# Bulk loads and stores of x issued by ScalarE, and the row of the maxima sent before the reciprocals are spread

## What is computed

```python
x = x + _layernorm(_L0_attn_ref(_layernorm(x), W_qkv, b_qkv, W_out, b_out))
x = x + _layernorm(_L0_ffn_ref(_layernorm(x), weight, alpha, bias))
# attention: softmax(causal(q k^T / sqrt(8))) v, then W_out
# ffn: einsum('bsd,od->bso', input, ternary(weight) * alpha) + bias
```

## Time and profile before

| | |
|---|---|
| median of 3 runs | 443.43 us |
| the profiled execution | 442.58 us |
| its span | 440.8 us |
| busy: PE, DVE, ACT, POOL | 375.1, 357.8, 329.5, 301.7 us |
| DMA queue of SP: packets, MB | 70880, 37.70 |
| DMA queue of ACT: packets, MB | 1336, 0.66 |
| mean granted clock of TensorE | 0.96 |

### The profile page before, as it was taken

How to read it: one execution, slowest core, us unless ns; L and a number is a source line. 1 busy time by engine, 2 the same in 40 slices (tenths; PEclk the granted TensorE clock), 3 DMA queues, 4 the chain that set the end, 5 groups by cost and what they waited for, 6 DMA issues and landing times.

```text
span 440.8 us, 19219 instructions
## 1 busy us (share of the span) xinstructions
PE 375.1 (85%) x7430; PEld 279.4 (63%) x7430; DVE 357.8 (81%) x1148; ACT 329.5 (75%) x609; POOL 301.7 (68%) x584
## 2 busy tenths in 40 slices
PE   0635898899999989998999999999989999998541
PEld 0323666567777767776777777777767777665230
DVE  5845775799999897998999998989989988985542
ACT  0412675788899887998989998898889889778521
POOL 2633332576888876888888887878887777656855
PEclk9998898999999998999999999999999999999955
DMA  7298545533344433333344334353345334511161
GB/s 192 42 122 96 91 104 116 123 82 84 80 85 85 83 76 74 83 82 76 75 87 85 83 85 86 80 123 84 85 84 126 83 82 85 113 45 33 56 188 48
DMA packets 72306, 39.58 MB, mean 90 GB/s; under 512 B 13048, under 2 KB 68056, under 8 KB 72216
## 3 DMA queue, kind: packets, MB, share of 16 engines
q1 hardware_dynamic: 70880, 37.70, 40.9%
q10 hardware_dynamic: 1336, 0.66, 0.6%
HBM read 13.67 MB, written 4.72 MB: 42 GB/s over the span
## 4 chain that ended last, share of the span: by engine, by line
PE 32%; DMA 25%; SPq 13%; issue 9%; DVE 8%; ACT 8%; POOL 5%; POOLq 0%; ACTq 0%; DVEq 0%
DMA QS<-MpT 9%; PE ps_st L795 7%; PE ps_mx L846 7%; DMA den<-Y 7%; PE ps_y L819 7%; SPq L260 6%; DMA rec_dram<-rec 4%; DMA QS<-part 4%; SPq L270 3%; ACT PT L427 3%; PE ps_w L875 3%; DVE M L627 3%; PE ps_w L916 3%; PE ps_w L905 2%; POOL rstd L358 2%
## 5 line engine op out<-in xcount | busy, mean ns | idle before, releaser
L627 DVE TENSOR_REDUCE M<-ps_mx 128x2 f32<-128x512 f32 (+3 forms) x352 | 211.9, 633 | 32.2 <-PE ps_mx L846 31.6
L427 ACT ACTIVATE PT<-ps_st 128x1024 f32<-128x1024 f32 (+1 forms) x192 | 162.6, 883 | 21.9 <-PE ps_st L795 15.8
L846 PE MATMUL ps_mx<-KS,QS 112*64 112x128 bf16 (+2 forms) x2560 | 136.9, 226 | 13.2 <-DMA QS<-part 10.3
L846 PEld LDWEIGHTS ps_mx<-KS,QS 112*64 112x64 bf16 x2560 | 94.1, 112 | 47.2 <-DVE M L627 13.1
L795 PE MATMUL ps_st<-QS,KS 114*64 114x256 bf16 (+1 forms) x1024 | 103.6, 304 | 13.6 <-DMA QS<-MpT 12.7
L358 POOL TENSOR_TENSOR rstd<-vareps,mhalf 128x2 f32<-128x2 f32 x128 | 91.7, 717 | 10.0
L819 PE MATMUL ps_y<-PT,VB 128*32 128x256 f32 (+3 forms) x2048 | 90.4, 303 | 0.4 <-ACT PT L427 0.3
L795 PEld LDWEIGHTS ps_st<-QS,KS 114*64 114x64 bf16 x1024 | 48.5, 111 | 20.5 <-DMA QS<-MpT 17.9
L819 PEld LDWEIGHTS ps_y<-PT,VB 128*32 128x32 f32 x2048 | 49.6, 109 | 12.9 <-issue 5.7
L400 POOL TENSOR_TENSOR rest<-QK,part 128x512 f32<-128x512 f32 x32 | 38.8, 1214 | 24.4 <-ACT part L456 24.4
L386 POOL TENSOR_TENSOR yn<-Y,rden 128x512 f32<-128x512 f32 x32 | 40.7, 1272 | 16.6 <-DMA rden<-rec_dram 16.6
(11 more groups left out here) (63 smaller groups left out, 492.2 us busy)
## 6 DMA issues: line engine op xcount, KB each, us to landing
QS<-part SPq DMA_DIRECT2D x192, 64.0 KB
rden<-rec_dram SPq DMA_DIRECT2D x32, 256.0 KB
X<-in_x SPq DMA_DIRECT2D x7, 512.0 KB, 5.4
out<-X SPq DMA_DIRECT2D x7, 512.0 KB, 4.4
KS<-part SPq DMA_DIRECT2D x32, 96.0 KB
KS<-part SPq DMA_DIRECT2D x32, 64.0 KB
KS<-part SPq DMA_DIRECT2D x32, 32.0 KB
QS<-MpT SPq DMA_DIRECT2D x32, 16.0 KB
```

The lines of the kernel that those rows point to most:

```text
L427: nc.scalar.activation(PT[(b * CHUNKS + n) % TILES][:, 0:512 * banks], ps_st[n % 2][:, 0:banks, :].rearrange("p a c -> p (a c)"), ACT.Exp, ...
L627: nc.vector.tensor_reduce(M[b % 2][:].rearrange("p k g i -> p (k g) i")[:, 2 * kv:2 * kv + pairs, i], ps_mx[(b * BANKS + n) % 2][:, 0:pair ...
L846: last = pe.matmul(ps_mx[(b * BANKS + n) % 2][64 * one:64 * one + 64, at:at + w], q[:, h, BL * i:BL * i + BL], k[:, kv, blocks, :], start= ...
```

## The change

Two things are done. First, `load_x` and `store_x` go from SP to ACT, with their DMAs on ACT's queue. On ACT the load stands first in a step; the store stands behind `take_xn1(t)` and takes batch t-10 in the place of t-21. ACT's loop gets two steps more and a last wait for all stores; SP's loop ends at t = 36. Second, SP's step sends the row of the maxima before it spreads the reciprocals.

```diff
         @block.sync
-            def load(g):
-                sp.dma_start(rows(g), xv[bass.ds(g, 1)].rearrange("n p r d -> (n p) r d")).then_inc(s_x, 16)
...
             def step(t):
-                load_x(t)
+                send_max(t - 3)
                 spread_rec(t - 5)
-                send_max(t - 3)
                 q_rows(t - 1, 1, 1)
                 q_rows(t - 1, 1, 5)
                 k_rows(t - 1, 2)
                 q_rows(t - 1, 2, 0)
-                store_x(t - 21)
                 send_den(t - 4)
...
-            for t in range(B + 21):
+            for t in range(B + 5):
                 step(t)
-
-            sp.wait_ge(s_store, 16 * (B // GRP - 1 + GRP))
...
         @block.scalar
+            def load_x(t):
+                g = t + 1
+                if g < B // GRP:
+
+                    act.wait_ge(s_x, g * 16)
+                    act.dma_start(rows(g), xv[g]).then_inc(s_x, 16)
+
+            def store_x(b):
+                if on(b) and (b % GRP == GRP - 1 or b >= B - GRP):
+
+                    act.wait_ge(s_fin, b + 1)
+                    if b < B - GRP:
+                        g = b // GRP
+                        act.dma_start(ov[g], rows(g)).then_inc(s_store, 16)
+                    else:
+                        at = (b - (B - GRP)) * TT
+                        act.dma_start(ov[B // GRP - 1, :, at:at + TT, :], X[:, TT * b:TT * b + TT, :]).then_inc(s_store, 16)
...
             def step(t):
+                load_x(t)
                 take_xn1(t)
+                store_x(t - 10)
                 exp(t - 4, 5)
...
-            for t in range(B + 8):
+            for t in range(B + 10):
                 step(t)
+
+            act.wait_ge(s_store, 16 * (B // GRP - 1 + GRP))
```

More of the change, by code:

```diff
@@ L224, in _ @@
             xv = x.rearrange("(n b) (j p) d -> n p (b j) d", b=GRP, p=128)
-            ov = out.rearrange("(n b) (j p) d -> n p (b j) d", b=GRP, p=128)
-            def rows(g):
-                return X[:, bass.ds(g * (GRP * TT), GRP * TT), :]
-            def load(g):
-                sp.dma_start(rows(g), xv[bass.ds(g, 1)].rearrange("n p r d -> (n p) r d")).then_inc(s_x, 16)
             sp.dma_start(X[:, 0:TT, :], xv[0, :, 0:TT, :]).then_inc(s_x0, 16)
@@ L239, in _ @@
                 sp.dma_start(dst[:], src).then_inc(s_late, 16)
[L241 to L246, removed]
             def rows_free(b):
@@ L418, in _, with rows @@
         def _(act):
+            xv = x.rearrange("(n b) (j p) d -> n p (b j) d", b=GRP, p=128)
+            ov = out.rearrange("(n b) (j p) d -> n p (b j) d", b=GRP, p=128)
+            def rows(g):
+                return X[:, bass.ds(g * (GRP * TT), GRP * TT), :]
             def exp(b, n):
```

## The result

The changed kernel takes 473.36 us in the median of 4 runs (469.52 to 476.2), against 442.77 us for the kernel before in its 4 runs: a ratio of 1.071, interval 1.064 to 1.078. It is 30.6 us slower. The forecast was 437.0 us, with a range to 448.

The account below looks back on a forecast made before the run. PE was taken to set the pace, with DVE close behind. Terms -9.5 - 1.7 + 4.2 - 2.4 + 3.3 + 0.5 = -5.6 us against 442.58 gave 437.0 us, range 428 to 448.

Parts of the forecast that it names:

- What is queued behind the row pays: On SP's queue, rden, part sends and den go out later behind the row: 0.2 us a step, +4.2 us, bounds 0 and +23.
- The 2.9 us of the earlier trace: Issue-to-use time of one den transfer of 16 KB without the spreading before it, compared with the row's 4.17 us.
- the 0.8 us for each store: Three group stores on SP directly ahead of a den each delay it by 0.8 us; moving them saves 2.4 us.
- the 1.0 us a step that was taken: DVE's distance behind PE in a steady step: a step takes 11.50 us, of which DVE needs 10.5.
- slower: Rival at send_max: SP stands at the row while rden and den wait; 0.85 us a step, 450.7 us, chance 0.15.
- The row goes first: Row sent before the spreading, 1.3 to 1.9 us earlier: PE's waits for it give -9.5 us, the slow clock stretch -1.7.
- Stores and loads on ACT: Stores meeting the spreading +3.3 us, stores no longer ahead of den on SP -2.4, ACT's issues of loads and stores +0.5.
- the cover named for its issues: ACT's waits for QK, 23.5 us together, hide its load and store issues; without that cover they would cost 9.2 us.
- the signs listed for "wrong": Most steps: yn waits for rden or reciprocal over 0.8 us for den; ACT's QK wait gone; or MpT waits that stay.

Follow-up runs that it names:

- e3_small: Changed kernel with the spreading of the reciprocals cut from 256 KB to 16 KB, most of the division left out: 448.99 us, ratio 1.014.
- e7_issue: Kernel before with one more DMA of 16 bytes on SP behind the row in each of 32 steps: 454.69 us, ratio 1.021.
- e2_move: Changed kernel with the two sends back in their old order, so only loads and stores move to ACT's queue: 451.37 us, ratio 1.008.
- e5_row_act: Kernel before with the row of the maxima sent by ACT on its own queue, behind the layer norm: 466.61 us, ratio 1.033.
- e6_row_act_move: Changed kernel with the row of the maxima sent by ACT on its queue, behind the layer norm: 460.20 us, ratio 1.031.
- e9_row_act_first: Kernel before with the row sent by ACT directly behind the copy of MpT, ahead of the layer norm: 465.21 us, ratio 1.046.

## Why the prediction was wrong

**The step that failed** is "What is queued behind the row pays". It bounded the loss at den by one issue, 0.66 us, and the loss at yn by 0.45, and took 0.2 us a step near the lower end, +4.2 us in all. Measured are 12.54 - 11.50 = 1.04 us a step, or +21.9 us in the steady part, and 5.0 us more in the ramp and the tail, where no loss was counted. Two things were missing in it. The first is the transfer: I counted the 256 KB only where they had stood before the row (1.3 us gained) and not where they went, ahead of the part sends and of den. Den's landing went from 3.6 us to 4.7 in the middle, while its issue moved by less than 0.1 us against MpT's copy, and e3_small shows that four fifths of the loss hang on these bytes. The second is the closed ring. I compared waits one by one and asked whether SP had room (it idled 18.5 + 14.1 us at the two sends). But that idle time was part of a loop that came back to SP by den, take_a, ff, turn and the copy, and this loop was closed already in 6 of 20 turns, of 11.0 to 11.6 us against a mean step of 11.50. It had some tenths of a microsecond of room, whatever SP's idle time.

One reading in the sum was off too. The 2.9 us of the earlier trace rows was taken as den's usual landing; it is the shortest of the nine between 120 and 360 us in which the reciprocal waited. Against the usual 3.6 the row's 4.17 us is 0.6 us late behind the spreading and not 1.3, and 4.17 for the den behind a store is well within 2.9 to 4.2, so the 0.8 us for each store rests on nothing firm. DVE was also nearer to PE than the 1.0 us a step that was taken: by busy time 232.88 against 220.29 us, or 0.6.

**The rival "slower"** had the place and the sign: SP stands at send_max while rden and den wait. It was priced at 0.85 us a step (450.7 us) and given 0.15. Its price was taken from the same bound of 1.1 us, without the transfer. That the measured 1.04 lies just under this bound is luck: the bound was 0.66 us for an issue and 0.45 for yn, and what came was 1.1 us of den's landing. The time still came out 23 us above 450.7; about half of that are the 9.5 and 1.7 us of gains that the case kept and that a step set by the ring can't give. e7_issue shows that even 0.65 us in this place costs 9 us.

**The row goes first: the waits went, and it was worth nothing.** The wait of st for MpT fell from 12.7 to 3.7 us (under 3 was forecast), and the slow stretch of the clock in the steady part is gone. But -9.5 and -1.7 us were to be had only if PE set the pace. With a step of 12.5 us, PE's saved waits came back as waits for yn (20.2 us) and for the parts (19.9, before 10.3). That the row lands sooner, in 2.9 us, is not seen: in the four places where PE still waited for it, all in ramp and tail, it was used 4.1 to 5.0 us after its issue, as before (3.1 to 5.2 over the whole span). The waits may have gone because the row is sent before the spreading, or because the longer step brings PE there later; no run separates the two.

**Stores and loads on ACT: small, as said.** +3.3, -2.4 and +0.5 us make +1.4; e2_move gives a ratio of 1.008, 3.6 us, inside the bounds. No run separates the three terms. ACT's wait for QK did not move (23.5 to 23.2 us), so the cover named for its issues held.

**What was to show it.** Of the signs listed for "wrong", the first came true in both its forms: yn waits for rden in nearly every step, and the reciprocal waits for den 1.9 us on average in 30 steps. I had also written that for the slower case "the reciprocal waits for den in nearly half of the steps already". That sentence deserved more weight than 0.15: a wait that shows up in half of the steps is a sign that the loop it belongs to is about as long as the step.

## What to carry to other kernels

In a hand-ordered pipeline, before moving a send ahead of another, follow the send's own product all the way round until it comes back to the same queue, and add up issues, landings and work: if the sum is near the step's length, each microsecond put into that loop is paid in every step, however idle the queue looks. A large transfer that is moved out of the way of one small one lands in the way of the next; price it at its new place too. Where several loops of nearly the same length share a stretch, cutting one shows little (4 us here, within noise), and the same cut shows its worth (15.5 us) only once the shared stretch is short.

## What the runs showed of the hardware that was not expected

- A queue of its own did not protect a small transfer. The row of 16 KB was used 4.5 to 5.7 us after its issue on ACT's queue, against 3.8 to 5.2 behind 256 KB on SP's, and den's landing stayed at 4.9 us when the 256 KB went by ACT's queue (30.5 us of waits in 240).
- The cost of the spreading rose faster than its bytes: ratio 1.014 with 16 KB, 1.021 with 128 KB, 1.071 with 256 KB, with den's landing at 4.0, 4.1 and 4.7 us.
- A DMA that ACT's list has behind a norm did not wait for the norm: it began 0.03 us after the end of the copy it needed (e5_row_act, e6_row_act_move). Placed ahead of the norm, it held the norm up by 0.76 us (e9_row_act_first).
- A send of 16 bytes cost as much of SP's time as one of 64 KB: e7_issue's chain has 0.65 us for it, and 0.63 to 0.65 for the part sends behind it. 9 us of the 21 so added reached the end.
